# Preparing one weight product of a cross-attention and feed-forward kernel: vector-engine transposes and 32-row strips in place of TensorE transposes and full-height matmuls

## The reference

```
x = x + Attn(layernorm(x))      # 8 heads of 128; keys and values from 154 context rows
x = x + FFN(layernorm(x))

Attn:  q = x Wq;  k = ctx Wk;  v = ctx Wv                    (Wq 512x1024, Wk and Wv 384x1024)
       sim = q k^T / sqrt(128);  sim = (sim - mean_j sim) * 1.5 + mean_j sim
       out = softmax(sim) v Wout + bout
FFN:   xr, xk = mixes of x with the row before it (weights mu_r, mu_k)
       out = sigmoid(xr W_r^T) * (relu(xk W_k^T)^2 W_v^T)
```

## Time and profile before

| | us |
|---|---|
| Median of three runs | 742.6 (742.1 to 742.7) |
| The profiled execution | 743.74 |
| Its span, first to last instruction | 741.9 |
| PE busy | 734.0 |
| PEld busy | 625.2 |
| DVE busy | 535.4 |
| ACT busy | 422.4 |
| POOL busy | 135.3 |

### The profile page before, as it was taken

How to read it: one execution, slowest core, us unless ns; L and a number is a source line. 1 busy time by engine, 2 the same in 40 slices (tenths; PEclk the granted TensorE clock), 3 DMA queues, 4 the chain that set the end, 5 groups by cost and what they waited for, 6 DMA issues and landing times.

```text
span 741.9 us, 13209 instructions
## 1 busy us (share of the span) xinstructions
PE 734.0 (99%) x3568; PEld 625.2 (84%) x3568; DVE 535.4 (72%) x1116; ACT 422.4 (57%) x1204; POOL 135.3 (18%) x314
## 2 busy tenths in 40 slices
PE   9999999999999999999999999999999999999998
PEld 8967887888888888888888888888888888888876
DVE  2688988786677767766777776677768667776755
ACT  3577866665556556556655655556566555655332
POOL 1111101222211212221021222112212221120311
PEclk9999999999999999999999999999999999999999
DMA  9976745554555555455555554455545454544312
GB/s 329 251 156 172 212 136 178 160 181 157 180 158 166 167 172 157 158 171 160 169 160 175 152 180 156 157 170 168 177 150 173 153 181 152 173 149 146 114 57 86
DMA packets 109559, 122.78 MB, mean 165 GB/s; under 512 B 12479, under 2 KB 82521, under 8 KB 109531
## 3 DMA queue, kind: packets, MB, share of 16 engines
q1 hardware_dynamic: 109492, 122.41, 53.7%
q10 hardware_dynamic: 39, 0.04, 0.0%
HBM read 66.83 MB, written 55.57 MB: 165 GB/s over the span
## 4 chain that ended last, share of the span: by engine, by line
PE 81%; SPq 6%; DVE 4%; ACT 2%; issue 2%; DMA 2%; POOL 1%; POOLq 0%; DVEq 0%; ACTq 0%
PE ffn L514 11%; PE ffn L516 11%; PE ffn L515 11%; PE scores L515 8%; PE scores L516 8%; PE scores L514 8%; PE attended L514 8%; PE attended L515 8%; PE attended L516 8%; SPq L349 3%; SPq L332 1%; DMA x_rows<-normed 1%; ACT probs L809 1%; PE attended L564 1%; PE attended L563 1%
## 5 line engine op out<-in xcount | busy, mean ns | idle before, releaser
L514 PE MATMUL scores<-A_hi,xT_hi 128*128 128x462 f32 x372 | 129.9, 349 | 0.6 <-DVE B_lo L1027 0.6
L515 PE MATMUL scores<-A_lo,xT_hi 128*128 128x462 f32 x372 | 130.1, 350 | 0.0
L516 PE MATMUL scores<-A_hi,xT_lo 128*128 128x462 f32 x372 | 129.8, 349 | 0.0
L514 PE MATMUL attended<-B_hi,pT_hi 128*128 128x512 f32 x288 | 112.9, 392 | 2.0 <-DVE pT_lo L1027 2.0
L515 PE MATMUL attended<-B_lo,pT_hi 128*128 128x512 f32 x288 | 113.0, 392 | 0.0
L516 PE MATMUL attended<-B_hi,pT_lo 128*128 128x512 f32 x288 | 113.0, 392 | 0.0
L809 ACT ACTIVATE probs<-scores,neg_max 128x154 f32<-128x154 f32 x248 | 93.6, 386 | 27.2 <-DVE neg_max L1101 27.2
L1415 POOL TENSOR_SCALAR var<-stats 128x1 f32<-128x1 f32 x64 | 13.3, 208 | 411.4 <-DVE stats L1033 411.4
L1101 DVE TENSOR_REDUCE neg_max<-scores 128x3 f32<-128x462 f32 (+1 forms) x93 | 53.4, 579 | 44.7 <-PE scores L516 44.7
L799 ACT CAST xT_hi<-xT 128x512 fp32r<-128x512 f32 x30 | 18.7, 623 | 107.7 <-DVE xT L1047 107.5
L514 PEld LDWEIGHTS scores<-A_hi,xT_hi 128*128 128x128 f32 x372 | 70.0, 188 | 8.4 <-issue 1.5
(11 more groups left out here) (180 smaller groups left out, 1572.7 us busy)
## 6 DMA issues: line engine op xcount, KB each, us to landing
prob_rows<-probs SPq DMA_DIRECT2D x32, 704.0 KB, 3.2
probs_handed<-prob_rows SPq DMA_DIRECT2D x128, 176.0 KB, 3.4
x_rows<-normed SPq DMA_DIRECT2D x61, 256.0 KB, 2.0
handed<-x_rows SPq DMA_DIRECT2D x244, 64.0 KB, 1.9
x_in<-in_x SPq DMA_DIRECT2D x32, 256.0 KB, 2.6
square_rows<-act SPq DMA_DIRECT2D x31, 256.0 KB, 2.0
act_handed<-square_rows SPq DMA_DIRECT2D x124, 64.0 KB, 1.9
out<-x SPq DMA_DIRECT2D x31, 256.0 KB, 2.3
```

What stands on the lines that cost most here:

```text
L514: te.matmul(psum, left[0], right[0], start=first, stop=False)
L515: te.matmul(psum, left[0], right[1], start=False, stop=False)
L516: return te.matmul(psum, left[1], right[0], start=False, stop=last)
```

## The change

Parts in the opening:

- Wq is loaded as `wq[q*32+i, b, :] = Wq[b*32+i, q*256:(q+1)*256]`: rows in blocks of 32, columns in quarters. It comes in two halves of four DMAs, each 256 KB to 32 partitions in pieces of 1 KB; SP issues quarters 0 and 1, ACT quarters 2 and 3, between its copies of Wk.
- DVE turns it with eight 32x32-block transposes of 128x512 (`queries_turn`). The 32 PE transposes, their eight copies and their four banks go.
- In `wqT` a slot now holds 32 rows of each of four heads. Wk is copied into the same order (`wk_slots`): per chunk ACT copies four slots and DVE four.
- A is 32 matmuls per chunk rather than 8: each with 32 contracted rows (strip q of the array), 128 output rows and 154 columns. Strip q writes bank q, accumulating over four slots. The cast and the subtraction of a chunk are in four pieces of 308 columns.
- `ctxT` gets a 155th column, the sum of the context over its rows, made by ACT's accumulation in three instructions rather than one copy. The key matmuls have 155 columns, and the sums of the keys come out as a column; the three reductions on DVE go.
- DVE's order is: `queries_turn(0, 0)`, shift, `queries_turn(0, 1)`, two shifts, four turns of chunks 1 and 2, statistics of tile 0, low parts of chunks 0 and 1, two turns of chunk 3, low part of chunk 2, statistics of tile 1, low part of chunk 3.

Orders changed elsewhere: the `mu` loads come after `hand_x(3)`; `normalise_late(1, 1)` after `pack_values()`; `x_root(6)` before `keep_halo(1, 1)` on POOL; in step 30 `squares(29)` after `probs_hi(31)` on ACT and `hand_x2(30)` before `store_squares(29)` on SP. `keep_halo` has a further wait for `halo_ready`.

```diff
-            wq_rows = Wq.rearrange("(c p) n -> p c n", p=P)
+            wq_rows = Wq.rearrange("(b i) (q n) -> q i b n", i=Q, q=4)
...
             for i in range(2):
-                cols = slice(4 * i * P, 4 * (i + 1) * P)
-                sp.dma_start(wq[:, :, cols], wq_rows[:, :, cols]).then_inc(wq_loaded[i], 16)
+                half = slice(2 * DC * i, 2 * DC * (i + 1))
+                for q in range(2):
+                    sp.dma_start(wq[q * Q:(q + 1) * Q, half, :], wq_rows[q][:, half, :]).then_inc(wq_loaded[i], 16)
...
             sp.dma_start(x_early[0][:], xt[4 * P:5 * P, :]).then_inc(early_loaded[0], 16)
+            store_x(3)
+            hand_probs(0)
+            hand_x(3)
             with nc.allow_non_contiguous_dma(reason="two vectors of 512 as columns"):
...
-            store_x(3)
-            hand_probs(0)
-            hand_x(3)
...
-                    for h in range(h0, h1):
-                        last = te.matmul(A_BANKS[c % 2][b][:, (h - h0) * J:(h - h0 + 1) * J],
-                                         wqT[:, h, c * P:(c + 1) * P], kT[:, h, :], start=True, stop=True)
-                    last.then_inc(A_done, 1)
+                    te.wait_ge(A_ready, 4 * (c - 1))
+                for e in range(2):
+                    te.wait_ge(wq_turned, 2 * c + e + 1)
+                    for b in range(4):
+                        slot = 4 * e + b
+                        if c == 0:
+                            te.wait_ge(kT_ready, 3 if e or b == 3 else slot // HPB + 1)
+                        for q in range(4):
+                            rows = slice(q * Q, (q + 1) * Q)
+                            last = te.matmul(A_BANKS[c % 2][q][:, e * J:(e + 1) * J],
+                                             wqT[rows, slot, c * P:(c + 1) * P], kT[rows, slot, :],
+                                             start=b == 0, stop=b == 3)
+                last.then_inc(A_done, 1)
+            te.wait_ge(A_ready, 4 * (DC - 1))
             turn_x(0)
...
-                squares(t - 1)
+                if not is_last(t + 1):
+                    squares(t - 1)
                 if is_tile(t + 1):
                     for i in range(3):
                         probs_hi(t + 1, i)
+                if is_last(t + 1):
+                    squares(t - 1)
...
+            for c in range(CC):
+                nc.scalar.activation(ctxT[:, c, 0:J], XB[:, c * J:(c + 1) * J], ACT.Identity,
+                                     accum_out=ctxT[:, c, J:KJ]).then_inc(ctxT_ready, 1)
+            wq_rows = Wq.rearrange("(b i) (q n) -> q i b n", i=Q, q=4)
+            for c in range(CC):
+                act_e.wait_ge(wk_loaded[c], 16)
+                copy(wk_slots[:, c, 0:4, :].rearrange("p s (q i) -> p s q i", i=Q),
+                     wk[:, c, :].rearrange("p (q s i) -> p s q i", q=4, i=Q)[:, 0:4]).then_inc(wk_low_ready, 1)
+                if c:
+                    half = slice(2 * DC * (c - 1), 2 * DC * c)
+                    for q in range(2, 4):
+                        nc.scalar.dma_start(wq[q * Q:(q + 1) * Q, half, :], wq_rows[q][:, half, :]
+                                            ).then_inc(wq_loaded[c - 1], 16)
...
+            queries_turn(0, 0)
+            keys_shift(0)
+            queries_turn(0, 1)
+            keys_shift(1)
+            keys_shift(2)
+            for c in (1, 2):
+                for e in range(2):
+                    queries_turn(c, e)
             x_statistics(0, 0, 1)
-            for c in range(DC):
...
+            for c in range(2):
+                product_lo(c)
+            for e in range(2):
+                queries_turn(3, e)
+            product_lo(2)
+            x_statistics(1, 1, 1)
+            product_lo(3)
             x_lo(0)
...
-            normalise_late(1, 1)
             values_lo(8)
             pack_values()
+            normalise_late(1, 1)
             probs_turn(0)
```

More of the change, by code:

```diff
@@ L190, in xattn_ffn @@
         assert at_mix + size_of([P, HEADS, D]) <= at_gate
-        ctxT = sb("ctxT", [P, CC, J], at=at_probs_handed)
+        ctxT = sb("ctxT", [P, CC, KJ], at=at_probs_handed)
         x1T = (sb("x1T_hi", [P, DC, P], F32R, at=at_gate), sb("x1T_lo", [P, DC, P], F32R, at=at_gate + size_of([P, D])))
@@ L446, in step @@
                     store_x2(t)
+                if is_tile(t) and is_last(t + 1):
+                    hand_x2(t)
                 if is_tile(t - 1) and not is_last(t - 1):
                     store_squares(t - 1)
-                if is_tile(t) and not is_last(t):
+                if is_tile(t) and not is_last(t) and not is_last(t + 1):
                     hand_x2(t)
@@ L686, in _ @@
             keep_busy(2)
-            te.wait_ge(ctxT_ready, 1)
+            te.wait_ge(ctxT_ready, CC)
             for c in range(CC):
-                te.wait_ge(wk_loaded[c], 16)
-                for b, (h0, h1) in enumerate(HEAD_BANKS):
-                    for h in range(h0, h1):
-                        last = te.matmul(S[b][:, (h - h0) * J:(h - h0 + 1) * J], wk[:, c, h * P:(h + 1) * P],
-                                         ctxT[:, c, :], start=(c == 0 and h == h0), stop=(c == CC - 1 and h == h1 - 1))
+                for b, (s0, s1) in enumerate(HEAD_BANKS):
+                    for slot in range(s0, s1):
+                        te.wait_ge((wk_low_ready, wk_high_ready)[slot // 4], c + 1)
+                        last = te.matmul(S[b][:, (slot - s0) * KJ:(slot - s0 + 1) * KJ], wk_slots[:, c, slot, :],
+                                         ctxT[:, c, :], start=(c == 0 and slot == s0),
+                                         stop=(c == CC - 1 and slot == s1 - 1))
@@ L924, in _ @@
                 for h in range(h0, h1):
-                    last = nc.scalar.activation(kT[:, h, :], S[b][:, (h - h0) * J:(h - h0 + 1) * J], ACT.Identity,
+                    last = nc.scalar.activation(kT[:, h, :], S[b][:, (h - h0) * KJ:(h - h0) * KJ + J], ACT.Identity,
                                                 bias=key_shift[:, h:h + 1], scale=STRETCH * SCALE)
                 last.then_inc(kT_ready, 1)
-            for h in range(1, HEADS, 2):
-                act_e.wait_ge(wq_turned, h + 1)
-                copy(wqT[:, h, :], WQ_BANKS[h % len(WQ_BANKS)][:]).then_inc(wqT_odd_ready, 1)
             for c in range(DC):
-                for b, (h0, h1) in enumerate(HEAD_BANKS):
-                    act_e.wait_ge(A_done, 3 * c + b + 1)
-                    copy(A_hi[:, c, h0 * J:h1 * J], A_BANKS[c % 2][b][:, 0:(h1 - h0) * J]).then_inc(A_hi_ready, 1)
+                act_e.wait_ge(A_done, c + 1)
+                for q in range(4):
+                    copy(A_hi[:, c, q * QK:(q + 1) * QK], A_BANKS[c % 2][q][:, 0:QK]).then_inc(A_hi_ready, 1)
                 if c == 0:
@@ L1275, in _, with queries_turn @@
                                 ).then_inc(keys_shifted, 1)
[L1276 to L1286 removed]
+            def queries_turn(c, e):
+                dve.wait_ge(wq_loaded[c // 2], 64)
+                to = wqT[:, 4 * e:4 * e + 4, c * P:(c + 1) * P].rearrange("p b (r i) -> p r b i", i=Q)
+                rows = wq[:, 4 * c:4 * c + 4, e * P:(e + 1) * P].rearrange("p r (b i) -> p r b i", i=Q)
+                v.transpose(to, rows).then_inc(wq_turned, 1)
@@ new lines, in product_lo @@
+            def product_lo(c):
+                for q in range(4):
+                    dve.wait_ge(A_hi_ready, 4 * c + q + 1)
+                    low_part(A_lo[:, c, q * QK:(q + 1) * QK], A_BANKS[c % 2][q][:, 0:QK],
+                             A_hi[:, c, q * QK:(q + 1) * QK]).then_inc(A_ready, 1)
+            for c in range(CC):
+                dve.wait_ge(wk_loaded[c], 16)
+                v.tensor_copy(wk_slots[:, c, 4:8, :].rearrange("p s (q i) -> p s q i", i=Q),
+                              wk[:, c, :].rearrange("p (q s i) -> p s q i", q=4, i=Q)[:, 4:8]).then_inc(wk_high_ready, 1)
@@ L1507, in _ @@
             x2_root(2)
+            x_root(6)
             keep_halo(1, 1)
-            x_root(6)
             keep_halo(2, 1)
```

66 lines of the change are left out of this document (17 added, 49 removed).

## The result

The changed kernel takes **752.88 us** (752.15 to 753.61, four runs), the kernel before 742.65 on the same chip: ratio 1.0143, 95% interval 1.013 to 1.0155. The prediction was 740.4, with a range to 744.3; the time lies outside it, on the slow side.

The account below looks back on a forecast made before the run. PE was taken to bound the kernel, so only the opening, waits up to about 115 us and the tail's wait could pay. +0.8 - 0.6 - 1.2 - 1.2 = -2.2 gave 740.4 us against 742.6, range 738.2 to 744.3.

Parts of the forecast that it names:

- When W_q lands: Opening: W_q's second half lands at 17.0, bounds 14.9 and 20.0, at a mean rate near 300 GB/s.
- Rival B: W_q load: two queues don't help, quarters share 196 GB/s; landing 20.0, opening +3.8, time 743.4; chance 0.24.
- What follows T: Opening, DVE, ACT and PE work from W_q's landing to `scores(0)`: 17.0 us, giving 34.0 against 33.2, +0.8.
- rival C: Opening: clock falls after PE waits for DVE from near 22 to 24.7, costing 1.7; time 742.1; chance 0.12.
- Strips: Products A on PE: four strips share the array fully, 0.13 per four, 2.2 us per chunk.
- rival D: Products A on PE: strips' weight loads go one after another, 0.44 a four; +15.8, time 756.2; chance 0.08.
- `normalise_late`: Before `scores(2)`: moving `normalise_late(1, 1)` removes PE's wait of 0.6; -0.6, bounds 0 and -0.6.
- `mu` and the lead: After the opening: later `mu` loads let `hand_probs(0)` go earlier, DVE and ACT up to 2.0 ahead; -1.2, bounds 0 and -1.4.
- Rival E: Reorderings give nothing, as other waits stand right behind; only +0.8 and the tail remain, 742.2; chance 0.06.
- The tail: Moving `squares(29)` lets the casts `attend(31)` waits for go 1.15 earlier; -1.2, bounds -1.0 and -2.8.
- ACT's list held by its issues: Opening: ACT's four DMA issues might delay `kT` behind them; priced at nothing beyond 0.7, named as a sign of error.

Follow-up runs that it names:

- e1_sp_all: Changed kernel, but SP alone issues all eight quarter transfers of W_q, ahead of x_in(0): 743.93 us, ratio 1.0032 to the kernel before.
- e3_hold_wide: Changed kernel, but SP waits for all of W_q before issuing W_v and all loads behind it: 748.21 us, ratio 1.0084 to the kernel before.
- e2_act_first: Changed kernel, but ACT issues its four quarters of W_q at its start, behind ctx1: 743.54 us, ratio 1.0028 to the kernel before.
- e5_wide_1k: As e4_wide_wq, but W_q in pieces of 1 KB in place of 2 KB (times alone, output wrong): 741.17 us, ratio 0.9978 to the kernel before.
- e14_wv_1k: Changed kernel, but W_v loaded in four transfers of 256 columns, pieces of 1 KB not 4 KB: 748.88 us, ratio 1.0092 to the kernel before.
- e15_late_wide_wv_1k: As e10_late_wide, with W_v also loaded in pieces of 1 KB (times alone, output wrong): 741.80 us, ratio 0.9991 to the kernel before.
- e4_wide_wq: Changed kernel, but SP loads W_q over 128 partitions in two transfers, 2 KB pieces (output wrong): 742.14 us, ratio 1.0003 to the kernel before.
- e6_blocks: Changed kernel, but SP loads W_q as 16 blocks of 32 rows, each over all 128 partitions: 757.76 us, ratio 1.0202 to the kernel before.
- e10_late_wide: As e4_wide_wq, but ACT issues W_q's second half, at 7.7 (times alone, output wrong): 744.84 us, ratio 1.0029 to the kernel before.
- e8_orders_head: Kernel before plus the change's reorderings except the tail's two, opening as before: 739.55 us, ratio 0.9960 to the kernel before.
- e17_head_third: e8_orders_head run once more as a yardstick: 739.61 us, ratio 0.9966 to the kernel before.
- e7_orders: Kernel before plus all the change's reorderings, tail included, opening as before: 740.02 us, ratio 0.9961 to the kernel before.

## Why the prediction was wrong, point by point

- **When W_q lands**: this step failed, and it made nearly all of the error. T, the landing of W_q's second half, was priced at 17.0 with an upper bound of 20.0, and it was 27.93: +10.9. Two assumptions were behind it. The mean rate near 300 for two queues: two queues of quarters share 185 to 192. And the bound itself: it took W_q as the only traffic, in one train at 196. In fact ACT's 1 MB was issued when SP had put W_v and W_out, in larger pieces, into the same engines, and its share was 74 to 105 GB/s. How the +10.9 divides: with one queue at 197 GB/s e1_sp_all is at 18.89, 1.9 over the 17.0. Its train starts at W_k's end of 8.22, the changed kernel's at 10.25, another 2.0. The 7.0 left are the wide loads beside ACT's quarters; taking them away gave back 4.7 in e3_hold_wide, 6.4 with its later W_k allowed for. Rival B had the first half of this (T = 20.0; e1_sp_all is 18.89). No rival had the second. It stood in the diff: SP's list goes straight from its quarters to W_v, and ACT's quarters come behind the second copy of W_k.
- **What follows T**: right. T + 17.0 came out as 17.2, and as 16.7, 17.3, 16.7, 17.2 and 17.2 in e1_sp_all, e2_act_first, e5_wide_1k, e14_wv_1k and e15_late_wide_wv_1k. In e4_wide_wq (20.8) it was more, for `kT` and PE's own gaps; in e3_hold_wide (18.5), e6_blocks (18.0) and e10_late_wide (17.9) for the clock, see rival C.
- **Strips, and rival D**: strips were priced right, at 0.13 a four. Fours of the changed kernel, two in a row at a granted clock of 0.50, and the first and last of fifteen at the high clock:

```profile
25.24 0.50 PE L718 MATMUL ffn<-kT,wqT 32*128 32x154 f32 x3
...
25.50 0.50 PE L718 MATMUL ffn<-kT,wqT 32*128 32x154 f32 x3
...
28.77 0.31 PE L718 MATMUL scores<-kT,wqT 32*128 32x154 f32 x3
...
30.61 0.31 PE L718 MATMUL scores<-kT,wqT 32*128 32x154 f32 x3
```

  One four every 0.26 at 1.2 GHz and (30.61 - 28.77) / 14 = 0.13 at 2.4 GHz. Rival D is refuted. Of the 3.07 of the Trainium skill, "TensorE: Matmul & The Clock Gate", "Measured speedup vs the span model", which the prediction quotes, nothing is seen: four strips cost as much as one full matmul.
- **The clock, rival C**: it fell, in the opening and not where C had it: during the idle time of 11.2, to 0.50 from 20 to 28. In the changed kernel it costs little, as PE would wait for W_q's second half anyway: the last four of chunk 1 starts at 30.61, about when DVE is through with its statistics. Where no such wait covers it, it costs what C feared, a little less: in e10_late_wide PE is idle for 4.67, the clock falls, and chunk 2 runs at half speed, so that DVE waits 1.11 for its cast.

```profile
24.00:28.00 4.00, 4.00 (x64) 0.50 1.21 209
...
28.74 1.25 DVE L1031 TENSOR_TENSOR A_lo<-ffn,A_hi 128x308 fp32r<-128x308 f32 x3 [1.11 <-ACT A_hi L938]
```

  e6_blocks has the same wait of 1.11 after PE was idle for 8.91, and e3_hold_wide one of 1.93, for chunk 0, after 7.92. C was priced at 1.7; by T + 17.2 these three lost 0.7 to 1.3.
- **`normalise_late`** -0.6 and **`mu` and the lead** -1.2: right in sum in the changed kernel, from `scores(0)` to `scores(31)` -2.2 against -1.8. In e8_orders_head the first shows only in part: a wait of 0.80 for `B_lo` stands inside `values_out` instead (there is none in e17_head_third, the same kernel). Rival E is refuted: the orders alone give 2.0 to 2.8.
- **The tail** -1.2: wrong in its mechanism, and nearly nothing in size. PE's wait was taken for the path; tile 30's rows on their way through DRAM to DVE were it. I wrote that "DVE's unmoved work on tile 30 is then late", as a bound, where it was the rule. The fall of the clock behind the earlier trace rows does not follow from that wait either: e8_orders_head has the same wait, 1.80, and a granted clock of 1.00. The 1.4 by which the kernel before is over 30.3 is about the size of that fall in its profiled execution, so part of this profile's tail was probably never there to be gained in the median; one trace alone has the fall.
- **ACT's list held by its issues**: it was not; the issues took 1.09 and 0.82.

The sum with T as measured, +0.8 + 10.9 - 1.8 = +9.9 with nothing for the tail, comes near the measured +10.2.

## What to carry to other kernels

A transfer's landing is not its size over a rate: list what the other queues have put into the same DMA engines by the time it is issued, with partitions and pieces (here two queues divided the bytes as their piece sizes), and let what is needed first be issued first, ahead of bulk loads of any queue. Before a layout is chosen for the engine that reads it, price its load: 32 partitions at a time nearly halved the rate here, whichever queues issued them. A wait on the busiest engine is on the path only if the next input it needs is not fixed by another chain; take a later landmark's distance to the end in several traces and see which one stays constant.

## What the runs showed of the hardware that I had not expected

- Two queues that write opposite halves of the partitions at the same time reach 185 to 192 GB/s together, one queue 197; over 128 partitions the same 1 KB pieces run at 349 (2 KB: 397 in a window of e4_wide_wq).
- Two queues with work got through equal numbers of pieces, 132 and 132, 272 and 275, 142 and 139, 244 and 249 in four windows of 2 us; so 1 KB pieces beside 4 KB ones moved 0.12 MB of 0.65.
- A transfer of 128 partitions whose outermost size is 4 keeps the DMA share at 0.27 and 96 GB/s.
- The four issues of `hand_x2(30)` took 2.92 us on SP in the changed kernel and 1.74 in e7_orders, where the same instructions stand in the same order. One of them alone took 1.31 in place of 0.43, and tile 30's rows came 1.2 later, counted from `scores(31)`. All kernels with the changed opening had one issue of 1.2 to 1.8 in this place. Why is open, as are PE's two gaps in e4_wide_wq, and why W_k, issued alike, landed anywhere from 8.22 (e1_sp_all) to 11.96 (e3_hold_wide).
